# Attention in an AdaLN block: every even head's second fp32 key tile becomes a split tile with a VectorE subtraction

## What is computed

```
scores = jnp.einsum('bhsd,bhtd->bhst', q, k) * scale
attn = jax.nn.softmax(scores, axis=-1)
o = jnp.einsum('bhst,bhtd->bhsd', attn, v_c)
```

## Time and profile before

| | |
|---|---|
| median of 3 runs | 969.82 us (969.69 to 972.84) |
| profiled execution | 971.64 us, its span 969.9 us |
| TensorE matmul busy | 863.9 us (89%) |
| TensorE weight loads busy | 605.4 us (62%) |
| VectorE busy | 657.6 us (68%) |
| ScalarE busy | 563.7 us (58%) |
| GpSimd busy | 632.8 us (65%) |
| TensorE clock granted, mean | 0.948 |

### The profile page before, as it was taken

How to read it: one execution, slowest core, us unless ns; L and a number is a source line. 1 busy time by engine, 2 the same in 40 slices (tenths; PEclk the granted TensorE clock), 3 DMA queues, 4 the chain that set the end, 5 groups by cost and what they waited for, 6 DMA issues and landing times. The chain is left out here.

```text
span 969.9 us, 20135 instructions
## 1 busy us (share of the span) xinstructions
PE 863.9 (89%) x7974; PEld 605.4 (62%) x7974; DVE 657.6 (68%) x1254; ACT 563.7 (58%) x968; POOL 632.8 (65%) x450
## 2 busy tenths in 40 slices
PE   4896999999999999999999979860899999999995
PEld 1352466666666666666666768850477777677764
DVE  4847878787888788887888519842276567565743
ACT  3741667676767676776767735753547545744550
POOL 5207888888888888888888955786223543452342
PEclk9996799999999999999999979965799999999998
DMA  9911000000000000000000024378434534452110
GB/s 273 329 81 34 2 2 2 2 2 1 2 3 2 2 2 2 2 2 1 3 1 2 2 88 154 119 259 260 139 110 137 179 115 150 130 179 97 47 48 20
DMA packets 52368, 72.32 MB, mean 75 GB/s; under 512 B 11618, under 2 KB 44583, under 8 KB 52048
## 3 DMA queue, kind: packets, MB, share of 16 engines
q1 hardware_dynamic: 42322, 53.93, 17.0%
q0 software_dynamic: 7680, 16.87, 5.3%
q10 hardware_dynamic: 2272, 0.24, 0.2%
HBM read 46.76 MB, written 29.67 MB: 79 GB/s over the span
## 5 line engine op out<-in xcount | busy, mean ns | idle before, releaser
L801 POOL TENSOR_TENSOR prob_lo<-prob 128x1024 f16<-128x1024 f32 x208 | 390.4, 1895 | 60.1 <-ACT prob L773 59.6
L828 DVE TENSOR_REDUCE part_max<-x_ps 128x1 f32<-128x512 f32 x512 | 325.2, 682 | 78.8 <-PE x_ps L722 74.8
L773 ACT ACTIVATE prob<-st_ps 128x512 f32<-128x512 f32 x512 | 281.6, 595 | 114.0 <-PE st_ps L710 108.2
L722 PE MATMUL x_ps<-KX,CQ 98*128 98x512 f16 x512 | 204.2, 402 | 5.2 <-DVE part_max L828 2.3
L710 PE MATMUL st_ps<-CQ,KX 99*128 99x512 f16 x512 | 196.7, 385 | 2.8 <-ACT prob L773 1.5
L1299 POOL DMA_INDIRECT out<-yo,xb x48 | 47.7, 995 | 153.6 <-DVE yo L1406 150.6
L748 PE MATMUL acc_ps<-VV,prob 128*128 128x65 f16 x1664 | 128.9, 193 | 2.5 <-POOL prob_lo L801 2.5
L748 PE MATMUL acc_ps<-VV,prob_lo 128*128 128x65 f16 x1664 | 128.5, 193 | 0.0
L748 PEld LDWEIGHTS acc_ps<-VV,prob 128*128 128x128 bf16 x1664 | 116.5, 98 | 17.7 <-DVE both L847 5.0
L748 PEld LDWEIGHTS acc_ps<-VV,prob_lo 128*128 128x128 f16 x1664 | 108.9, 98 | 21.4
L1329 ACT ACTIVATE act_f<-g_ps,cols 128x768 f32<-128x768 f32 x64 | 57.7, 901 | 104.7 <-PE g_ps L1452 102.6
(11 more groups left out here) (172 smaller groups left out, 1267.1 us busy)
## 6 DMA issues: line engine op xcount, KB each, us to landing
w1f<-in_L_ffn_w SPq DMA_DIRECT2D x8, 1024.0 KB, 4.9
w2f<-in_L_ffn_w SPq DMA_DIRECT2D x8, 1024.0 KB
xbuf<-zeros SPq DMA_DIRECT2D x7, 910.0 KB, 17.1
xb<-xbuf SPq DMA_DIRECT2D x8, 780.0 KB
x<-in_L_attn_h_t SPq DMA_DIRECT2D x8, 512.0 KB, 9.2
out<-x SPq DMA_DIRECT2D x4, 1024.0 KB
tbuf<-x SPq DMA_DIRECT2D x4, 1024.0 KB
tbuf<-gb_row SPq DMA_DIRECT2D x4, 1024.0 KB
```

What stands on the lines that cost most here:

```text
L722: mm(x_ps[i % 3][:], queries_of[:, n % 2, b * P:(b + 1) * P, j], KX[0:QROWS, n % KRING, f * HALF:(f + 1) * HALF], start=True, stop=True).t ...
L773: nc.scalar.activation(prob[:, k, f * HALF:(f + 1) * HALF], st_ps[i % 2][:], ACT.Exp).then_inc(exp_done, 1)
L801: nc.gpsimd.tensor_tensor(prob_lo[:, k, :], prob[:, k, :], prob_top[:, k, :], ALU.subtract).then_inc(sub_pool, 1)
L828: nc.vector.tensor_reduce(part_max[:, n % 2, j, f:f + 1], x_ps[((n * ST + j) * 2 + f) % 3][:], AX.X, ALU.max).then_inc(smax_done, 1)
```

## The change

In even heads tile 6 is no longer whole. It is a split tile, and its subtraction is queued on VectorE, in slot 3 after that slot's two maxima (the scores of tile 6 are computed in slot 2, its values in slot 6). TensorE waits for a semaphore of its own, `sub_vector`, before this tile. GpSimd's subtractions stay as they are.

```
         def whole(n):
-            return (3,) if n % 2 else (1, 6)
+            return (3,) if n % 2 else (1,)
+
+        def by_vector(n):
+            return () if n % 2 else (6,)
 
         def by_pool(n):
-            return [k for k in range(ST) if k not in whole(n)]
+            return [k for k in range(ST) if k not in whole(n) + by_vector(n)]
...
-                    te.wait_ge(sub_pool, pool_before[n] + by_pool(n).index(k) + 1)
+                    if k in by_vector(n):
+                        te.wait_ge(sub_vector, n // 2 + 1)
+                    else:
+                        te.wait_ge(sub_pool, pool_before[n] + by_pool(n).index(k) + 1)
...
+                def subtract(n, k):
+                    v.wait_ge(exp_done, (n * ST + k) * 2 + 2)
+                    nc.vector.tensor_tensor(prob_lo[:, k, :], prob[:, k, :], prob_top[:, k, :],
+                                            ALU.subtract).then_inc(sub_vector, 1)
...
                         if k == ST - 1:
                             whole_rows(p + 2)
+                    ns, ks = scores_of(p, k - 1) if k else (-1, 0)
+                    if is_head(ns) and ks in by_vector(ns):
+                        subtract(ns, ks)
                     if k - 1 in KEY_SLOTS and is_head(p + 3):
                         keys_low(p + 3, KEY_SLOTS.index(k - 1))
```

## The result

| | before | changed |
|---|---|---|
| median of 6 runs | 970.6 us (969.69 to 972.84) | 975.3 us (974.05 to 976.15) |
| profiled execution | 971.64 us, span 969.9 | 974.05 us, span 972.3 |

The ratio is 1.0045, with a 95% interval of 1.003 to 1.0059: slower by 2.9 to 5.7 us. The prediction was +5.8 us.

What follows compares the result with a forecast made beforehand. TensorE sets the pace, limited by how far VectorE may lag through three banks. 15 even heads at +0.32 us give 4.8, plus 1.0 at the end: +5.8 us, 975.6 from the median 969.82; range 967 to 980 (8 in 10).

Steps and rivals of the forecast that it cites:

- What TensorE saves: Tile 6 of even heads, split instead of whole fp32: TensorE's own work falls by 1.23 us an even head.
- How long VectorE's subtraction takes: Slot 3 of even heads: 1.22 us alone, 1.95 us when held by GpSimd's subtraction of tile 7, ending at 325.13.
- Who waits: Slots 5 and 6 of even heads: TensorE waits 1.55 us more at the second maxima, slot 7 starting 0.32 us later.
- The walk: VectorE's queue followed by instruction from slot 3 to slot 7 of an even head: +0.32 us each.
- The next subtraction: GpSimd, behind VectorE's subtraction in even heads: loses about 0.5 us, taken up by 1.36 us of idle time, cost nothing.
- The end: From head 30, without row maxima and with GpSimd always busy: VectorE's subtraction holds GpSimd's next, +1.0 us.
- the second one: Attention stage, even heads: VectorE does not wait for GpSimd, each head gains 0.38 us, 964.1 us; chance 0.10.
- The stride: VectorE's subtraction in even heads: strided operand halves its rate, 1.07 us more a head, 993 us; chance 0.04.
- the additional waits: Slot 7 into slots 0 to 2 of odd heads: a further wait, 0.3 us a head more, 980 us; chance 0.05.
- The whole saving: Even heads: TensorE's saving comes through in full, 951.3 us; GpSimd's load was held against it; chance 0.03.
- the first rival: Even heads: VectorE is back earlier, small margin, -0.1 to +0.12 us a head, 968 to 972.7 us; chance 0.20.

Runs made afterwards that it cites:

- the values tile alone: Changed kernel with VectorE's subtraction left out from head 2 on, tile 6 of even heads still split; 953.9 us, ratio 0.9826 to the kernel before.
- the first experiment: Changed kernel with VectorE's subtraction of tile 6 moved to the end of slot 2, ahead of GpSimd's of tile 7; 965.0 us, ratio 0.9942 to the kernel before.
- the last kernel: Subtraction of tile 5 on VectorE instead of tile 6, plus 11 of 14 subtractions of heads 30 and 31; 947.6 us, ratio 0.9758 to the kernel before.

## Why the prediction was right

**What TensorE saves.** 1.23 us an even head was predicted; the values tile alone gave 15.32 - 14.09 = 1.23.

**How long VectorE's subtraction takes.** 1.22 us alone, predicted from the two sizes of the earlier trace rows, measured 1.226 when it asks first. Held, 1.95 was predicted and 1.91 measured; the 0.04 come from VectorE's start, 0.03 us after the end of the maximum in front of it, which the sum had counted as part of the hold. Its end was predicted at 324.05 + 1.08, and it comes 1.08 us after the end of GpSimd's in every one of the 16 heads (1.078 to 1.083).

**Who waits.** The two waits of TensorE came in slots 5 and 6 at the second maximum. In the time of the earlier trace rows the first is at 326.44 - 0.66 = 325.78 (325.79 predicted), the second at 328.48 - 0.66 = 327.82 (327.84), and slot 7 starts at 329.24 - 0.66 = 328.58 (328.60). The head costs +0.30 us for +0.32.

**One step was right by luck.** The walk lets the first maximum of slot 4 start 0.08 us before the subtraction's end, as a maximum does behind another one, and gives no reason why it should do so behind a subtraction. In the trace of before the maximum behind VectorE's other two-operand instruction there, `keys_low`, starts 0.03 us after its end, 56 times of 56 in heads 1 to 29; the earlier trace rows has one of them, 324.82 + 0.69 = 325.51 against 325.55. With that value the walk would have said +0.43 us a head, and +7.5 for the whole. The maximum started at 325.70, 0.08 before 325.78; in the first experiment it was 0.03 after.

**GpSimd.** The next subtraction was held for 0.53 us, 0.5 predicted, and the idle time after it took that up: odd heads are unchanged.

**The end.** +0.97 for +1.0.

**The sum.** Attention from the end of head 0 to the end of head 31 went from 572.06 - 122.97 = 449.09 us to 575.70 - 122.18 = 453.52: +4.43 in the two profiled executions. The walk says 14 x 0.32 + 1.0 = 5.5 for this stretch, and 0.32 more for head 0. Of the difference of 1.1, 0.7 is in the kernel before, two of whose even heads (6 and 22) had a pause of 0.34 us between VectorE and TensorE early in the head, of which the prediction took no account; why they had it was not tried. Most of the rest is 0.02 us less a head. The medians are 4.7 us apart, the prediction had 5.8, and the interval of the measurement, 2.9 to 5.7, ends just below that. That the forecast of 975.6 us lies only 0.3 from the measured 975.3 is partly luck, since the median before moved from 969.8 with three runs to 970.6 with six. The two profiled executions are only 2.4 us apart: beside the +4.43 the changed one was 0.8 us shorter up to the end of head 0 and 1.2 us shorter behind the attention stage, where nothing was changed; why was not tried.

**The rivals.** That VectorE does not wait here (the second one) gives 964.1 us, and the first experiment shows that number when the order of arrival is turned round: 965.0. The stride (the fourth) is excluded by 1.226 us, the additional waits (the fifth) by odd heads of 14.09. The whole saving (the third) needed another place in VectorE's queue, and there GpSimd, which I held against it, was no bound. What the first rival said of the margin stands: 0.3 us of one instruction's end decided the sign, and with half of the subtraction the kernel was faster than before.

The rule of the Trainium skill on which the wait was weighed ("SBUF — State Buffer", section "Who interferes with whom") held in both directions: 1.91 us on VectorE and 2.42 on GpSimd when GpSimd starts first, 1.22 and 2.72 when VectorE does.

## What to carry to other kernels

An engine that feeds another through a few buffers has no use for idle time that comes too late, behind work on which the other waits: 1.9 us added some maxima ahead of 1.4 us of idle time cost 1.53 us, and a subtraction of 1.4 us put into an idle time of 1.3 us cost nothing. So don't ask how busy the helper is, but how long it may lag at the place of the new work, and walk the queue instruction by instruction from there to the next point at which it has caught up. When work moves to VectorE that reads two operands from SBUF, look up what GpSimd runs at that moment, not on average, and put it just ahead of GpSimd's instruction or into a stretch in which neither is waited for.

## What the runs showed of the hardware

- Two instructions of VectorE and GpSimd with two SBUF operands each take turns, whole instruction by whole instruction: VectorE's ended 1.08 us after GpSimd's, whether it had begun 0.30, 0.83 or 1.80 us ahead of that end, and one of 512 elements 0.55 us after it. In the head in which it waited 1.80 us, GpSimd's next subtraction had been queued directly behind the first, and VectorE, which came before that one, went first (2.88 us each).
- With one engine alone a tile's subtraction takes 1.23 us on VectorE and 1.89 on GpSimd. Since they take turns, one subtraction on VectorE lengthened four of GpSimd's from 7.45 to 8.43 us. Where nothing else needed VectorE, giving it 11 of 14 was worth 5.3 us in two heads.
- How soon VectorE starts its next instruction is not the same everywhere. The first maximum behind `keys_low`, which works on partitions from 64 on, starts 0.03 us after the end of what is in front of it: `keys_low` itself (56 times of 56 before), or the subtraction of the first experiment, which stands between the two (15 of 15). In the changed kernel two maxima stand between `keys_low` and the subtraction, and the maximum behind it starts 0.08 us before its end. That is 0.1 us a head and was not expected. That the subtraction was held there does not tell the cases apart: in the last kernel subtractions that were not held are followed by the next 0.07 to 0.08 us before their end too. The cause was not tried.
